# Moving the base rows and the second weights in the synchronous queue of a mixture-of-experts feed

## What is computed

```
x = layernorm(x + retention(x))            # layer 0, 8 heads
x = layernorm(x + cross_attention(x, ctx)) # 16 heads, 77 context rows
x = layernorm(x + routed(x) + shared(x))   # 64 experts of width 64, best 8 of them; 2 shared of width 512
x = layernorm(x + linear_attention(x))     # layer 1
x = layernorm(x + cross_attention(x, ctx))
x = layernorm(x + gated_experts(x))        # 8 experts of width 512, best 2 of them
```

## Time and profile before

| | us |
|---|---|
| median of 3 executions | 1845.67 |
| the profiled execution | 1841.33 |
| its span in the trace | 1838.7 |
| feed: last stores of attention 0 to last quad | about 510 to 1024 |
| TensorE busy, share of the span | 1614.6, 88% |
| VectorE, ScalarE, GpSimd busy | 1171.8, 626.1, 871.2 |

### The profile page before, as it was taken

How to read it: one execution, slowest core, us unless ns; L and a number is a source line. 1 busy time by engine, 2 the same in 40 slices (tenths; PEclk the granted TensorE clock), 3 DMA queues, 4 the chain that set the end, 5 groups by cost and what they waited for, 6 DMA issues and landing times.

```text
span 1838.7 us, 45517 instructions
## 1 busy us (share of the span) xinstructions
PE 1614.6 (88%) x17739; PEld 1297.2 (71%) x17739; DVE 1171.8 (64%) x3267; ACT 626.1 (34%) x957; POOL 871.2 (47%) x968
## 2 busy tenths in 40 slices
PE   6898988897787899989998789899872999999994
PEld 5676777776555677667676556677662999999994
DVE  4578777776421666777466678988762445556564
ACT  1333333333312675545555344445421111111110
POOL 0006777777783005788778776433333002222223
PEclk9999999998998899999999799999985999999997
DMA  9516656466688777888889732212216112333332
GB/s 322 191 39 210 216 190 207 154 217 213 204 230 234 268 281 269 301 294 275 303 292 348 252 102 88 79 60 81 109 51 199 45 58 88 93 98 92 97 100 66
DMA packets 207761, 322.40 MB, mean 175 GB/s; under 512 B 25035, under 2 KB 163135, under 8 KB 206783
## 3 DMA queue, kind: packets, MB, share of 16 engines
q1 hardware_dynamic: 171231, 226.01, 37.1%
q0 software_dynamic: 33024, 92.32, 15.5%
q10 hardware_dynamic: 3296, 1.17, 0.2%
HBM read 157.02 MB, written 162.40 MB: 174 GB/s over the span
## 4 chain that ended last, share of the span: by engine, by line
PE 64%; DVE 12%; POOL 8%; DMA 6%; issue 5%; ACT 4%; SPq 1%; ACTq 1%; DVEq 0%; POOLq 0%
PE wide L2152 14%; PE d_yp L2164 7%; PE wide L110 4%; PE wide L127 3%; PE bank L1102 3%; PE e_yp L1820 3%; POOL big L1515 3%; PE wide L1809 3%; PE wide L1268 3%; PE bank L1288 3%; PE e_xp L1797 3%; PE wide L1271 2%; PE wide L1255 2%; POOL lists L681 2%; PE bank L1281 2%
## 5 line engine op out<-in xcount | busy, mean ns | idle before, releaser
L1515 POOL DMA_INDIRECT big<-results,slots x256 | 272.1, 1063 | 214.1 <-DMA results<-e_y 131.7
L2152 PE MATMUL wide<-d_xt,d_ws 128*128 128x128 f32 x2272 | 278.2, 276 | 0.6 <-issue 0.6
L2152 PEld LDWEIGHTS wide<-d_xt,d_ws 128*128 128x128 f32 x2272 | 271.8, 193 | 4.5 <-issue 1.0
L681 POOL DMA_INDIRECT lists<-big,slots x160 | 158.7, 992 | 84.8 <-issue 38.8
L747 ACT ACTIVATE pt<-wide 77x2048 f32<-77x2048 f32 x64 | 119.8, 1871 | 131.0 <-PE wide L1271 128.1
L2052 ACT ACTIVATE d_gate<-wide 128x512 f32<-128x512 f32 x71 | 42.4, 597 | 326.2 <-PE wide L2152 326.2
L2017 POOL DMA_INDIRECT d_picked<-results,slots x64 | 63.4, 990 | 178.4 <-DMA results<-d_y 165.3
L2164 PE MATMUL d_yp<-d_wd,d_h 128*128 x568 | 134.2, 379 | 0.0
L127 PEld LDWEIGHTS wide<-shared_sw,shared_sh 128*128 128x128 f32 x512 | 98.1, 192 | 45.7 <-issue 29.7
L110 PE MATMUL wide<-shared_sx,shared_sw 128*128 128x512 f32 x256 | 127.6, 622 | 2.5 <-ACT shared_sh L118 2.5
L127 PE MATMUL wide<-shared_sw,shared_sh 128*128 128x256 f32 x512 | 122.9, 384 | 4.3 <-DVE big L1774 4.3
(11 more groups left out here) (294 smaller groups left out, 3359.3 us busy)
## 6 DMA issues: line engine op xcount, KB each, us to landing
lists<-zero SPq DMA_DIRECT2D x20, 2048.0 KB, 14.7
e_x<-lists SPq DMA_DIRECT2D x80, 512.0 KB
results<-e_y SPq DMA_DIRECT2D x80, 512.0 KB
d_x<-lists SPq DMA_DIRECT2D x71, 128.0 KB, 2.2
results<-d_y SPq DMA_DIRECT2D x71, 128.0 KB, 1.7
e_w<-in_L_w SPq DMA_DIRECT2D x2, 4096.0 KB, 39.9
shared_sw<-in_x_t SPq DMA_DIRECT2D x32, 128.0 KB, 3.8
x<-in_x SPq DMA_DIRECT2D x8, 512.0 KB, 4.1
```

What stands on the lines that cost most here:

```text
L681: pool.indirect_dma_start(out=lists, out_offset=bass.IndirectOffsetOnAxis(ap=slots[:, b, i, k:k + 1], axis=0), in_=z2[i % 3][:, b, :], in_ ...
L1515: pool.indirect_dma_start(out=picked[:, c % NG, b, :], out_offset=None, in_=results[0:-(-PAGES_OF_STEP[s] // 4) * 4 * R0, :], in_offset=ba ...
L2152: ins = mm(out[T % 2][:, a * P:(a + 1) * P], ws[:, T % NW, n, c, a * P:(a + 1) * P], xt[:, T % 2, c], start=c == 0, stop=c == KC - 1)
```

## The change

The base rows' two transfers are made two jobs. `send` n only stores, and a new job `reload` n loads the rows of step n+1, still behind a wait for the store. For n of 2 to 6, `send` moves two quads on and `reload` stands two quads behind that; `reload` 1 stands behind quad 1; send 0 keeps its load. The units of the first 24 quads move from behind quads 5, 11, 17 and 23 to 8, 13, 18 and 23. The first `load_w2` is issued with the shared experts' rows of the third step (step 2), ahead of send 0.

```diff
@@ feed_order, L1375 @@
-            units(1 if j % 6 == 5 else 0)
+            units(1 if j in (8, 13, 18, 23) else 0)
@@ L1387 @@
     sums(STEPS * K0)
+    order.insert(order.index(("quad", 1)) + 1, ("reload", 1))
+    for n in range(2, STEPS - 1):
+        at = order.index(("send", n))
+        quads = [job[1] for job in order[at:] if job[0] == "quad"]
+        order.remove(("send", n))
+        order.insert(order.index(("quad", quads[1])) + 1, ("send", n))
+        order.insert(order.index(("quad", quads[3])) + 1, ("reload", n))
@@ SyncE's part of feed_phase, L1623 @@
                     experts.load_rows(sp, src_t, shared)
                     shared += 1
+                    if n == UNITS:
+                        load_w2(0)
                 if kind == "send":
                     send_base(n)
-                    if n + 1 < STEPS:
-                        load_rows(n + 1)
                     if n == 0:
-                        load_w2(0)
+                        load_rows(1)
+                    if n == 0:
                         load_w2(1)
+                if kind == "reload":
+                    load_rows(n + 1)
```

## The result

The changed kernel took 1823.77 us (median of 4 executions, 1820.37 to 1825.47) against 1846.32 of the kernel before: 22.5 us less, ratio 0.9871, 95% interval 0.985 to 0.9892. In a second series, 6 executions of it gave 1826.67 against 1847.2, ratio 0.9884, interval 0.9852 to 0.9917. Forecast were 18 us and 1827.7, with a range of 1822 to 1840: the time lies in the range, and 0.2 us outside the band of 1824 to 1832 that was given a chance of 0.50.

The account below looks back on a forecast made before the run. The kernel was taken as mostly bound by TensorE, losing time where SyncE's waits made transfers late. Gains 4 + 7 + 6 + 1 = 18 us took the median from 1845.67 to 1827.7, range 1822 to 1840.

Parts of the forecast that it names:

- The first half earlier: Start: first half of second weights asked for 8.3 us earlier, second half landing only 1 us earlier, at 578.
- rival 4: Start: halves strung out, the second landing at 609 if one takes 50.8 us; 6 us slower, 1851.7; chance 0.07.
- TensorE had ended its units at 565.6: Start, kernel before: TensorE's units were taken as finished at 565.6, well before quad 0's rows landed at 586.9.
- the cover of the early half: Start: TensorE ending about 574 instead of 565.6 costs nothing, since quad 0 can't begin before 580; otherwise 8 us paid.
- the unit-17 wait: Start: unit 17 would start at 551.8 but TensorE waits 5 us for base 1, whose rows land about 555.
- Load of rows 2 behind quad 1: Start: SyncE no longer waits for send 1; quad 0's rows land at 583 instead of 586.9.
- The term of the start: Up to quad 0: gain 4 us, taken between 0 and 7.
- Quads 0 to 23: Of 12.0 us lost there, 9.4 at quad 6, small waits leave 5; gain 7, bounds -2 to 12.
- Rival 1: Quads 0 to 23: transfers take over, 1 of the 7 us remains; gain 12, 1833.7; chance alone 0.17.
- Place three: Near send 4: router's rows asked for earlier, VectorE's wait under 1 us instead of 5.46; gain 6, bounds 0 to 6.8.
- Rival 2: Place three stays: VectorE's chain late by itself or GpSimd can't follow; gain 12, 1833.7; chance 0.12 with or without rival 1.
- Behind the feed: After the feed nothing is edited; GpSimd must follow, and the whole gain is carried to the end.

Follow-up runs that it names:

- e6: Changed kernel with both halves of the second weights ahead of send 0, against the changed kernel; 1841.78 us against 1826.67.
- after, again: The changed kernel (after) traced once more, unedited (again), against the kernel before; 1826.67 us, ratio 0.9884.
- e7: Changed kernel with the units back behind quads 5, 11, 17 and 23; 1824.31 us, ratio 0.9884 to the kernel before.
- e4: Changed kernel with sends 3 to 6 whole again (send, wait, load in one place); 1832.88 us, ratio 0.993 to the kernel before.
- e9: Changed kernel with reload 1 behind quad 6 instead of quad 1; 1826.53 us, ratio 0.9882 to the kernel before.
- e1: Kernel before with only the first half of the second weights asked for early; 1843.55 us against 1846.41.
- e2: Changed kernel without the early half and with units at their old places, so only the split against the kernel before; 1833.36 us against 1846.41.
- e5: Changed kernel with both halves of the second weights behind send 0; 1826.46 us, ratio 0.989 to the kernel before.
- e10: Kernel before with only sends 3 to 6 split from their loads and moved; 1840.15 us against 1846.49.

## Why the prediction was right, and where it wasn't

**The sum.** By the means over traces: start 85.2 to 79.5, quads 0 to 23 98.4 to 89.0, behind that 330.7 to 323.2, together 5.7 + 9.4 + 7.5 = 22.6 us, beside the measured 22.5. So close a match is chance: two traces of one kernel differ by up to 4.5 us in a stretch, and the first pair of traces alone gives 20.4. Forecast were 4, 7 and 7: every term had the right sign and place, and every one was too small.

**The first half earlier.** Right in the balance: I said 1 us for the landing and the traces show about 1.3, though it was asked for 8.3 us earlier. The send was held as expected, from 528.7 to 552.9. The rule of the Trainium skill named in the prediction ("DMA: Bandwidth & Descriptors", section on queues, rings and completion order), that each DMA engine takes one ring's descriptors in order, agrees with this trace and with e6: the small store didn't pass the weights, with one half ahead or with two. The bound of 609, rival 4, didn't happen: strung out, each half took 27.1 and 28.2 us here, and 27.0 to 30.0 in the six traces that have them so. About 50 us a half takes only with the other half ahead of it in the queue (49.7 to 52.3), with both late or, in e6, both early. One reading of the prediction was off: the long issues ended 12.6 and 10.6 us ahead of a landing (556.8 - 544.2, 579.4 - 568.8), not "11 to 12"; nothing in the sum hangs on it.

**The step that failed** is "TensorE had ended its units at 565.6". The chain of waits leaves TensorE for SyncE there, and I took that for the end of TensorE's work. It worked on until 577.6. Its own rows in the kernel before, and the window 570 to 580, say so:

```profile
575.72 1.89 PE L127 MATMUL wide<-shared_sw,shared_sh 128*128 128x256 f32 x8
587.02 1.94 PE L1797 MATMUL e_xp<-ident,e_x 128*128 128x128 f32 x8 [9.41 <-DMA e_x<-lists]
570.00:580.00 10.00, 7.61 (x28) 4.86 (x26) 0.23 (x1) 1.37 (x2) 0.00 (x0) 1.00 1.00 253
```

So the cover of the early half was 9 us and not 21, and the first turn stood in danger: the unit-17 wait, forecast at 5 us, was 0, 2.2, 2.9, 3.3 and 3.3 in the five traces with the change's start (after, again, e7, e4, e9), and in e4 TensorE's own work set the first turn, at 70.5. That it did no harm at store 0 was luck: the wait was smaller than expected, and three things end close together there, in the first trace GpSimd's copies (62.8, plus 5 for the rows), TensorE (64.5), and the weights (64.1, plus 4 for staging, which nobody waits for: the first product starts at 73.1). The chain of waits names the copies and the rows, so with the changed kernel GpSimd's last copies, not the weights, are what quad 0 waits for.

**Load of rows 2 behind quad 1.** Right: quad 0's rows were asked for at 62.9, where GpSimd's copies landed (forecast 577 on before's scale, 63.6), and the turn came at 68.0 (forecast 69.6). The term of the start measured 5.9 us in this pair of traces, 5.7 by the means, instead of 4. That the two edits help each other was not forecast: alone they bring 0.5 (e1) and 2.8 us (e2, e5 at store 0), together 5.7. With both, quad 0's rows are on their way 3.7 to 7.8 us instead of 7.1 and 8.2 with the split alone (DMA `e_x<-lists` in the chains; e4's doesn't stand in one), and TensorE, kept later by the unit-17 wait, has less idle time and less of the slow clock behind it. With traces that differ by 3 us this account is likely, not shown.

**Quads 0 to 23.** Right in mechanism; the loss before was 12.7 by the mean and not 12.0; the small waits were 3.0 us (88.73 - 85.7) where I said 5. The wait for transfers came early, 1.81 us at quad 5's rows, and e9 names the load behind it. The split with the units at their old places (e2 and e7, mean 91.8) brings 6.6 us, about the 7 forecast for all; the 2.8 us of the units' places were not in my sum as a term of their own. Rival 1, transfers taking over, didn't come: 306 GB/s over the whole stretch.

**Place three.** Right: 6 plus 1 forecast, 7.5 by the means (5.5 in the pair of first traces, since before's was a low one). e4 and e10 undo and do it alone, with the same rows. One reading was off: VectorE's wait, forecast under 1 us, is 1.3 to 2.7; TensorE's is nearly gone all the same (0.84 or less). Rival 2 falls: the wait at place three was for the router's rows, and it went with them.

**Behind the feed** all was carried: 815.6 and 816.3 us, within the 810.2 to 816.5 of all traces.

## What to carry to other kernels

Where a queue serves a stream that an engine needs every few microseconds, put no wait for a landing in it: issue the store at one place and the load that depends on it some turns later. An early request in the same queue, behind which a small transfer must pass (send 0: 24 us behind one half, 36 behind two), moves that transfer to the end of the large one; ask who needs the small one. And read the end of an engine's work from its own timeline, not from where the chain leaves it.

## What the runs showed of the hardware that was not expected

How slowly TensorE starts again goes with how long it stood at quad 0's first turn, but not by that alone. The turn took 1.94 us (1.2 GHz) after idle times of 3.55, 5.67 and more, but 1.06 (2.4 GHz) after 0.73 (after, again) and 1.79 us (e7), and 1.18 after 2.41 (e9); there the second turn, behind a wait of 1.29 us for ScalarE, was the slow one. After no idle time (e4, e6) both ran at full speed, 8.8 us from first turn to store 0 instead of 10.2 to 12.0. At unit 17 the same length went both ways (1.89 us is the group's time at full clock): behind 2.21 us of idle time it took 3.61 (after, again), behind 3.33 it took 3.78 (e4), but behind 3.34 only 1.99 (e9).

```profile
562.67 3.78 PE L127 MATMUL wide<-shared_sw,shared_sh 128*128 128x256 f32 x8 [3.33 <-DVE big L1786]
563.75 1.99 PE L127 MATMUL wide<-shared_sw,shared_sh 128*128 128x256 f32 x8 [3.34 <-DVE big L1784]
```

What decides at equal idle times stays open. The shorter idle time ahead of quad 0 fits the 1.2 us that the early half gains between first turn and store 0 (e5); no run separates it.

SyncE's issue of a small DMA right behind a 4 MB one takes long: 11.02 us for send 0 behind one half, 24.01 behind two, 20.4 for the first of the shared rows behind two, where an issue with nothing large ahead takes 0.3 to 0.6. In these three it ended 11.2, 9.6 and 10.6 us ahead of the landing of the last half ahead of it, so it looks as if the queue takes the next DMA only once the large one has been drawn in for the most part.
